# Middle units numbered by chunk, the first bias transposed by TensorE, another order on VectorE in the first layer, and two of four shared rounded copies made by VectorE

## The chip, the cores and the metric

The kernel runs on one core of one Trainium2 chip. The time is device microseconds of one execution; three executions of the kernel before gave 276.58, 276.78 and 278.21 us, median 276.78. The profile is of a fourth execution, taken by the hardware profiler.

## The reference

Two layers with residuals, for 32 batches of 128 tokens with 128 features. What is computed, cut to its core:

```python
# layer 0: a dense layer plus a low-rank term that differs by batch
z = ((x @ v) / 128) @ u.T / 16                # u = v = fside, 128 x 16 per batch
x = x + gelu(x @ W.T + fc_bias + z + cond)    # exact gelu
# layer 1: a gate picks 2 of 4 experts per batch, and a shared expert is always added
logits = gate_in @ gate_w + gate_b            # gate_in: three means over token segments of x
w_be = top-2 softmax weights of logits * (1 + scale) + shift     # scale, shift from cond
for e in range(4):                            # expert 1 skips one token segment, expert 2 another
    h = gelu_tanh(x @ ew1[e] + eb1[e])        # 128 -> 512
    out += w_be[e] * mask[e] * (h @ ew2[e] + eb2[e])             # 512 -> 128
x = x + out + (gelu_tanh(x @ sw1 + sb1) @ sw2 + sb2)
```

The order of the 512 middle units is free, as long as the first weights' columns, the first bias and the second weights' rows agree.

## The kernel before, in words

Features lie on the partitions. The 32 batches are 8 tiles of 4 batches (512 token columns). Tokens are reordered into three segments so that each expert reads one contiguous range: the shared expert (s = 0) and experts s = 1 and 4 take 512 columns per tile, s = 2 and 3 take 344.

Every product of layer 1 is done as three matmuls of values split into a rounded part and a rest (lines 449 to 451, `product3`: high by high, low by high, high by low). So each weight matrix is rounded by ScalarE (`weight_high`, line 323) and its rest is taken by VectorE (`weight_low`, line 679), and each middle activation `h` is split into `hs_hi` and `hs_lo`.

The work of layer 1 is a list `STEPS` of (tile, expert). It begins (0,0), (1,0), then the four experts of tile 0, then (2,0), the four experts of tile 1, (3,0), and so on: a round is four expert steps and one shared step. A step k has three parts:

- `up(k)` on TensorE: 4 chunks of 128 middle units, three matmuls each, into a ring of five PSUM banks. Chunk n waits until ScalarE has finished chunk n-5 (`h_ok`). TensorE runs `up` two steps ahead of `down`.
- `gelu(k)` on ScalarE: one activation per chunk into `h` (line 373). In a shared step a second activation per chunk writes the rounded `hs_hi` straight from PSUM (line 376). Before a shared step it waits until `down(k-2)` is done (line 370), as that frees `hs_hi`; before any step it waits for the split of step k-3 (line 368).
- `split(k)` on VectorE: for an expert `hs_hi` = h * w_be (line 695) and `hs_lo` (line 700), four instructions each; for a shared step only `hs_lo`, two instructions over two chunks each (line 689). Then `down(k)` on TensorE waits for `lo_ok`.

Layer 0 is done for tiles 0 to 3 ahead of layer 1 (xT, transpose_F, matrices, layer0 on TensorE; matrix, residual on VectorE; gelu0 on ScalarE). The first layers of tiles 4 to 7 are woven into rounds 0 to 3 (`late_tile`). In those rounds ScalarE loads another activation table, does `gelu0_late` (lines 354 to 361) and loads the first table again, right behind the shared step. The gate of tiles 0 to 3 is computed by VectorE (`segment_sums`, `time_gate`, `gate_in`, `modulation`, `gate_logits`, `gate_weights`, `output_biases`) with two small matmuls (lines 604 and 576) and one tanh on ScalarE; tiles 4, 5 and 6, 7 follow in later rounds.

Each engine's instructions stand in the order in which the code writes them, and wait by semaphores; nothing is reordered. SyncE issues nearly all loads in one queue: inputs, then weights in the order `WEIGHTS = [0, 1, 2, 4, 3, 6, 5, 8, 7, 9]` (2s is the first matrix of expert s, 2s+1 the second). Middle unit numbers are p * 4 + c for chunk c: the first matrices are read with a stride of four elements (line 201), and each partition of a second matrix is one run of 2 KB (line 249). GpSimd adds the output biases to `x1`, three instructions per tile (line 308), as soon as `output_biases` of the tile's gate group is done; `out_sum(t)` on VectorE waits for them.

## Time and profile before

| | |
|---|---|
| median of three runs | 276.78 us |
| profiled execution | 276.94 us, of which its span 274.8 us |
| TensorE (PE) busy | 244.4 us, 89% |
| VectorE (DVE) busy | 198.8 us, 72% |
| ScalarE (ACT) busy | 156.2 us, 57% |
| GpSimd (POOL) busy | 22.2 us, 8% |
| mean granted TensorE clock | 0.958 of 2.4 GHz |

How to read it: the profile cuts the span in 40 slices of 6.9 us and gives each engine's busy share and the granted clock of TensorE by slice in tenths. The timeline of one engine lists its instructions in order with the idle time before each and the engine that ended it. TensorE's modelled busy time reaches past the start of the next matmul; the distance from start to start is what a matmul costs in a stream.

### The profile page before, as it was taken

Reading aid. Unit: us, or ns where it says so; the run is one execution under the profiler, and the core shown is the slowest. Engines: PE = TensorE matmul, PEld = TensorE weight load, DVE = VectorE, ACT = ScalarE, POOL = GpSimd, SP = SyncE. Lnnn points to the kernel's source line nnn. Section 1 sums busy time; section 2 is a strip of 40 time slices with the busy share of each in tenths; the row PEclk is TensorE's granted clock in tenths of the full one; section 3 lists DMA queues with packets and bytes.
Section 4 is the critical chain, followed back from the end, with each engine's and each line's share of the span. In section 5 each row is a group of like instructions: output and inputs, shape, how many; then the busy total and the mean of one; then the engine's idle time right before and its main releaser. Section 6 shows DMA issues by size and latency. Waiting matters only on the chain.

```text
span 274.8 us, 3451 instructions
## 1 busy us (share of the span) xinstructions
PE 244.4 (89%) x1217; PEld 203.2 (74%) x1217; DVE 198.8 (72%) x441; ACT 156.2 (57%) x286; POOL 22.2 (8%) x39
## 2 busy tenths in 40 slices
PE   8964969799979997999989997999979989999963
PEld 7763748678768875888768885887768959898852
DVE  0266799999369565797399795797499959779661
ACT  4375799630894439760894439751835194544400
POOL 5000000940000000000000060000000600000000
PEclk9995598999999999999999999999999999999987
DMA  6995000000001000010001000010001000100101
GB/s 129 235 284 96 1 1 0 0 2 0 0 2 38 0 0 4 6 32 2 1 0 38 2 0 0 6 36 0 0 0 41 0 0 0 43 0 0 38 0 38
DMA packets 15811, 7.40 MB, mean 27 GB/s; under 512 B 6175, under 2 KB 14515, under 8 KB 15795
## 3 DMA queue, kind: packets, MB, share of 16 engines
q1 hardware_dynamic: 14781, 6.98, 10.6%
q10 hardware_dynamic: 854, 0.18, 0.3%
q8 instruction: 9, 0.15, 0.2%
q0 software_dynamic: 160, 0.02, 0.1%
q14 instruction: 7, 0.06, 0.1%
HBM read 5.09 MB, written 2.10 MB: 26 GB/s over the span
## 4 chain that ended last, share of the span: by engine, by line
PE 61%; ACT 16%; DVE 14%; issue 4%; DMA 2%; SPq 2%; DVEq 0%; ACTq 0%
PE ps L449 19%; PE ps L451 17%; PE ps L450 17%; ACT h L373 5%; ACT hs_hi L376 4%; DVE hs_lo L700 4%; DVE hs_hi L695 3%; PE ps L496 2%; DMA x_tok<-in_x 2%; DVE W_lo L679 2%; ACT L373 2%; ACT L354 2%; PE ps L508 2%; DVE hs_lo L689 2%; ACT W_raw L359 2%
## 5 line engine op out<-in xcount | busy, mean ns | idle before, releaser
L373 ACT ACTIVATE h<-ps,b_col 128x512 f32<-128x512 f32 (+1 forms) x160 | 94.1, 649 | 60.5 <-PE ps L451 38.4
L700 DVE SCALAR_TENSOR_TENSOR hs_lo<-h,w_be,hs_hi 128x512 fp32r<-128x512 f32 (+1 forms) x128 | 78.4, 673 | 0.0
L449 PE MATMUL ps<-x_hi,W_hi 128*128 128x512 f32 (+1 forms) x160 | 65.1, 407 | 14.2 <-ACT h L373 5.5
L449 PE MATMUL ps<-hs_hi,W_hi 128*128 128x512 f32 (+1 forms) x160 | 59.9, 375 | 6.3 <-DVE hs_lo L700 4.9
L695 DVE TENSOR_SCALAR hs_hi<-h,w_be 128x512 fp32r<-128x512 f32 (+1 forms) x128 | 50.3, 455 | 13.7 <-ACT h L373 6.9
L451 PE MATMUL ps<-x_lo,W_hi 128*128 128x512 f32 (+1 forms) x160 | 60.0, 375 | 0.0
L450 PE MATMUL ps<-x_hi,W_lo 128*128 128x512 f32 (+1 forms) x160 | 59.8, 374 | 0.0
L451 PE MATMUL ps<-hs_lo,W_hi 128*128 128x512 f32 (+1 forms) x160 | 59.0, 369 | 0.0
L450 PE MATMUL ps<-hs_hi,W_lo 128*128 128x512 f32 (+1 forms) x160 | 59.0, 369 | 0.0
L449 PEld LDWEIGHTS ps<-x_hi,W_hi 128*128 128x128 f32 x160 | 30.8, 192 | 27.9 <-ACT hs_hi L376 10.8
L449 PEld LDWEIGHTS ps<-hs_hi,W_hi 128*128 128x128 f32 x160 | 30.6, 191 | 11.6 <-DVE hs_lo L700 2.8
L689 DVE TENSOR_TENSOR hs_lo<-h,hs_hi 128x1024 fp32r<-128x1024 f32 x16 | 18.9, 1221 | 24.8 <-ACT hs_hi L376 24.8
L451 PEld LDWEIGHTS ps<-x_lo,W_hi 128*128 128x128 f32 x160 | 30.9, 193 | 4.5
L308 POOL TENSOR_TENSOR x<-x,bias 128x168 f32<-128x168 f32 (+1 forms) x24 | 18.2, 789 | 196.6 <-DVE bias L812 196.6
L451 PEld LDWEIGHTS ps<-hs_lo,W_hi 128*128 128x128 f32 x160 | 30.6, 191 | 4.3
L450 PEld LDWEIGHTS ps<-hs_hi,W_lo 128*128 128x128 f32 x160 | 30.7, 192 | 4.2
L450 PEld LDWEIGHTS ps<-x_hi,W_lo 128*128 128x128 f32 x160 | 31.1, 194 | 3.1
L376 ACT ACTIVATE hs_hi<-ps,b_col 128x512 fp32r<-128x512 f32 x32 | 22.8, 711 | 0.0
L391 ACT ACTIVATE x_tok<-ps 128x512 f32<-128x512 f32 x8 | 4.8, 598 | 28.6 <-PE ps L562 28.6
L327 ACT ACTIVATE x<-ps 128x512 f32<-128x512 f32 x8 | 4.8, 597 | 17.9 <-PE ps L466 17.9
L712 DVE TENSOR_TENSOR outT<-ps,x 128x168 f32<-128x168 f32 (+1 forms) x24 | 6.5, 327 | 5.3 <-PE ps L451 5.2
L654 DVE SCALAR_TENSOR_TENSOR h<-ps,WT 128x512 f32<-128x512 f32 x4 | 2.8, 689 | 9.3 <-PE ps L496 9.3
(102 smaller groups left out, 173.4 us busy)
## 6 DMA issues: line engine op xcount, KB each, us to landing
W_raw<-in_L_cond_ew SPq DMA_DIRECT2D x8, 256.0 KB, 4.9
out<-x_tok SPq DMA_DIRECT2D x8, 256.0 KB, 2.3
x_tok<-in_x SPq DMA_DIRECT2D x6, 168.0 KB
x_tok<-in_x SPq DMA_DIRECT2D x3, 176.0 KB
W_raw<-in_L_cond_sw SPq DMA_DIRECT2D x2, 256.0 KB, 5.0
x_tok<-in_x SPq DMA_DIRECT2D x3, 84.0 KB
F_raw<-in_fside_Bx1x1024x SPq DMA_DIRECT2D x3, 64.0 KB, 5.3
x_tok<-in_x SPq DMA_DIRECT2D x2, 88.0 KB
```

Source lines behind the costliest of these rows:

```text
L308: nc.gpsimd.tensor_tensor(xb[:, :, at:at + n], xb[:, :, at:at + n], bias2[:, i, t * NB:(t + 1) * NB].unsqueeze(2).to_broadcast([128, NB, n ...
L354: nc.scalar.activation(table_probe[:, 1:2], table_probe[:, 0:1], ACT.Gelu)
L359: ins = nc.scalar.activation(g0_late[:, b * L:(b + 1) * L], psLate[:, b * L:(b + 1) * L], ACT.Gelu, bias=bias0[:, t * NB + b:t * NB + b + 1])
L373: ins = nc.scalar.activation(span(h[:, k % 3, c, :], s), up_bank(k, c), ACT.Gelu_apprx_tanh, bias=b1_col[:, s, c:c + 1])
L376: ins = nc.scalar.activation(hs_hi[:, k % 2, c, :], up_bank(k, c), ACT.Gelu_apprx_tanh, bias=b1_col[:, s, c:c + 1])
L449: nc.tensor.matmul(dst, w_hi, m_hi, start=start, stop=False)
L450: nc.tensor.matmul(dst, w_lo, m_hi, start=False, stop=False)
L451: return nc.tensor.matmul(dst, w_hi, m_lo, start=False, stop=stop)
L689: nc.vector.tensor_tensor(hs_lo[:, k % 2, c:c + 2, :], h[:, k % 3, c:c + 2, :], f32(hs_hi[:, k % 2, c:c + 2, :]), ALU.subtract).then_inc(l ...
L695: nc.vector.tensor_scalar(hs_hi[:, k % 2, :, c], h[:, k % 3, :, c], w_be[:, t * NB + b, s - 1:s], None, ALU.mult).then_inc(hi_ok, 1)
L700: nc.vector.scalar_tensor_tensor(hs_lo[:, k % 2, :, c], h[:, k % 3, :, c], w_be[:, t * NB + b, s - 1:s], f32(hs_hi[:, k % 2, :, c]), ALU.m ...
L712: nc.vector.tensor_tensor(dst_v[:, :, dst:dst + n], sum_v[:, :, at:at + n], x1_v[:, :, at:at + n], ALU.add).then_inc(outT_ok, 1)
```

## The change

Six edits:

1. Middle units are numbered c * 128 + p. The first matrices are then read contiguously by the casts; a second matrix is loaded as four runs of 512 B per partition.
2. The first biases are loaded as 20 rows of 512 B (`b1_rows`), earlier in SyncE's queue, transposed by TensorE into PSUM (behind the transpose of `eb2`), and copied into `b1_col` by VectorE.
3. VectorE's order in the first layer: the block `segment_sums(0, 2)`, `time_gate`, `output_rows` no longer stands ahead of the matrix of tile 3. `weight_low` of the first matrix, `x1_low` and others move with it; `output_biases(0)` moves behind the split of step 4; two `weight_low` now stand ahead of `gate_logits(0)`.
4. TensorE: six idle matmuls ahead of `up(0)`; the modulation matmul behind `up(0)` instead of ahead of it; `logits(0)` behind `up(1)` instead of `up(0)`. ScalarE rounds the fourth weight ahead of `gelu(0)` instead of behind `gate_tanh(0)`.
5. In a shared step ScalarE writes `hs_hi` of chunks 0 and 1 only; VectorE copies chunks 2 and 3 from `h` in one instruction of 1024 columns.
6. GpSimd's bias additions of tile t also wait until VectorE's split of the step two before the tile's first expert step is done.

```diff
-                return W1_raw[:, e, :].rearrange("p (m c) -> p c m", c=CH), W1_hi[:, e, :, :], W1_lo[:, e, :, :]
+                return W1_raw[:, e, :].rearrange("p (c m) -> p c m", c=CH), W1_hi[:, e, :, :], W1_lo[:, e, :, :]
...
-                    sp.dma_start(W2_raw[:, e, :], src.rearrange("(p c) d -> p (c d)", c=CH)).then_inc(w_in[n], 16)
+                    sp.dma_start(W2_raw[:, e, :].rearrange("p (c d) -> p c d", c=CH),
+                                 src.rearrange("(c p) d -> p c d", c=CH)).then_inc(w_in[n], 16)
...
             load_weight(WEIGHTS[0])
+            sp.dma_start(b1_rows[0:CH, :], sb1.rearrange("(c p) -> c p", c=CH)).then_inc(b1_in, 16)
+            sp.dma_start(b1_rows[CH:NS * CH, :], eb1.rearrange("e (c p) -> (e c) p", c=CH)).then_inc(b1_in, 16)
...
             for t in range(NT):
+
+                pool.wait_ge(lo_ok, parts_until(first_step(t) - 2))
                 pool.wait_ge(bias2_ok, next(g for g, (a, z) in enumerate(GATES) if a <= t < z) + 1)
...
-                    if s == 0:
+                    if s == 0 and c < CH // 2:
                         ins = nc.scalar.activation(hs_hi[:, k % 2, c, :], up_bank(k, c), ACT.Gelu_apprx_tanh,
...
-            act.wait_ge(b1_in, 32)
+            weight_high(WEIGHTS[3])
+            act.wait_ge(b1_ok, 1)
             gelu(0)
             gate_tanh(0)
-            weight_high(WEIGHTS[3])
             gelu(1)
...
+                    pe.wait_ge(b1_in, 16 * 2)
+                    nc.tensor.transpose(psB1, b1_rows[:, :], ident[0:NS * CH, 0:NS * CH]).then_inc(b1_ps, 1)
+
+            keep_busy(6, ps[:, 6, 0:128])
+            up(0)
             pe.wait_ge(eb2T_read, NSEG)
+            pe.wait_ge(b1_ok, 1)
             pe.wait_ge(mod_terms_ok, 1)
             nc.tensor.matmul(psMod, ones[:, :], mod_terms[:, :, :], start=True, stop=True).then_inc(mod_ps, 1)
-            up(0)
+            up(1)
             logits(0)
-            up(1)
...
                 if s == 0:
+
+                    nc.vector.tensor_copy(hs_hi[:, k % 2, CH // 2:, :], h[:, k % 3, CH // 2:, :]).then_inc(shared_hi_ok, 1)
                     for c in range(0, CH, 2):
+                        if c == CH // 2:
+                            dve.wait_ge(shared_hi_ok, t + 1)
...
+                dve.wait_ge(b1_ps, 1)
+                nc.vector.tensor_copy(b1_col[:, :, :], psB1.rearrange("p (s c) -> p s c", c=CH)).then_inc(b1_ok, 1)
...
-                if t == 1:
+                if t == 2:
+                    output_rows()
+                    weight_low(WEIGHTS[0])
                     segment_sums(0, 2)
-                    time_gate()
-                    output_rows()
-            weight_low(WEIGHTS[0])
             segment_sums(2, 4)
+            time_gate()
             gate_in(0)
+            x1_low(NA - 1)
             dve.wait_ge(bias_in, 16 * 3)
             modulation()
-            x1_low(NA - 1)
-            gate_logits(0)
             weight_low(WEIGHTS[1])
             weight_low(WEIGHTS[2])
+            gate_logits(0)
...
-            output_biases(0)
...
+                if k == 4:
+                    output_biases(0)
```

Two places in the order of instructions. First VectorE in the first layer, before, from the rest of x1 of tile 0 on (`h<-ps,WT` is the matrix of a tile, `x<-x,h` its residual, `x_lo` the rest of its x1):

```order
L666 TENSOR_TENSOR x_lo<-x,x_hi 128x512
L673 TENSOR_REDUCE segsum<-x 128x8 x3
L717 SCALAR_TENSOR_TENSOR silu<-tanh_c,condT 128x32
L720 TENSOR_SCALAR tw<-time_w_raw 128x8
L722 TENSOR_TENSOR mod_terms<-silu,tw 128x256
...
L736 COPY eb2T<-ps 128x4 x3
L738 MEMSET eb2T 128x1
L739 MEMSET eb2T 128x1
L654 SCALAR_TENSOR_TENSOR h<-ps,WT 128x512
L661 TENSOR_TENSOR x<-x,h 128x512
L666 TENSOR_TENSOR x_lo<-x,x_hi 128x512
```

and the same place now:

```order
L678 TENSOR_TENSOR x_lo<-x,x_hi 128x512
L666 SCALAR_TENSOR_TENSOR h<-ps,WT 128x512
L673 TENSOR_TENSOR x<-x,h 128x512
L678 TENSOR_TENSOR x_lo<-x,x_hi 128x512
L752 COPY eb2T<-ps 128x4 x3
L754 COPY b_col<-ps 128x20
L756 MEMSET eb2T 128x1
L757 MEMSET eb2T 128x1
L691 TENSOR_TENSOR W_lo<-W_raw,W_hi 128x512
L685 TENSOR_REDUCE segsum<-x 128x8 x3
L673 TENSOR_TENSOR x<-x,h 128x512
```

The matrix of tile 3 (the `h<-ps,WT` row) now follows the rest of tile 0 directly, and the rest of the first weight stands ahead of all sums.

Second ScalarE around the first shared step, before, from the last cast of x1 on:

```order
L382 ACTIVATE x_hi<-x 128x512
L323 ACTIVATE W_hi<-W_raw 128x512
L373 ACT_TABLE_LOAD
L373 ACTIVATE h<-ps,b_col 128x512
L376 ACTIVATE hs_hi<-ps,b_col 128x512
L373 ACTIVATE h<-ps,b_col 128x512
L376 ACTIVATE hs_hi<-ps,b_col 128x512
L373 ACTIVATE h<-ps,b_col 128x512
L376 ACTIVATE hs_hi<-ps,b_col 128x512
L373 ACTIVATE h<-ps,b_col 128x512
L376 ACTIVATE hs_hi<-ps,b_col 128x512
L386 ACTIVATE tanh_g<-logit_x 128x64
```

and now:

```order
L389 ACTIVATE x_hi<-x 128x512
L330 ACTIVATE W_hi<-W_raw 128x512 x2
L380 ACT_TABLE_LOAD
L380 ACTIVATE h<-ps,b_col 128x512
L383 ACTIVATE hs_hi<-ps,b_col 128x512
L380 ACTIVATE h<-ps,b_col 128x512
L383 ACTIVATE hs_hi<-ps,b_col 128x512
L380 ACTIVATE h<-ps,b_col 128x512 x2
L393 ACTIVATE tanh_g<-logit_x 128x64
```

Six activations stand where eight stood, here and in each of the other seven shared steps, and one more weight is rounded ahead of them.

## Rows read from the trace of the kernel before

**Rows 1.** The page: granted TensorE clock in 40 slices, tenths of full speed.

```profile
PEclk9995598999999999999999999999999999999987
```

**Rows 2.** Timeline of TensorE: start, us, line, tiles, count, idle before and who ended it.

```profile
17.39 1.16 PE L508 MATMUL ps<-x,h 128*128 128x128 f32 x8
22.54 2.05 PE L508 MATMUL ps<-x,h 128*128 128x128 f32 x8 [3.99 <-issue]
...
28.12 0.80 PE L449 MATMUL ps<-x_hi,W_hi 128*128 128x512 f32 x1 [2.68 <-DVE W_lo L679]
...
55.59 0.47 PE L449 MATMUL ps<-hs_hi,W_hi 128*128 128x512 f32 x1 [2.37 <-DVE hs_lo L700]
```

**Rows 3.** Timeline of VectorE in the first 52 us.

```profile
18.73 1.33 DVE L673 TENSOR_REDUCE segsum<-x 128x8 f32<-128x336 f32 x3
...
21.74 0.69 DVE L654 SCALAR_TENSOR_TENSOR h<-ps,WT 128x512 f32<-128x512 f32 x1
...
25.79 0.69 DVE L661 TENSOR_TENSOR x<-x,h 128x512 f32<-128x512 f32 x1 [2.16 <-ACT h L348]
...
33.77 0.23 DVE L766 TENSOR_TENSOR logit<-ps,gate_mul 128x64 f32<-128x64 f32 x1 [1.69 <-PE ps L576]
...
46.76 0.69 DVE L679 TENSOR_TENSOR W_lo<-W_raw,W_hi 128x512 fp32r<-128x512 f32 x1
47.36 0.50 DVE L808 TENSOR_TENSOR gate_terms<-w_be,eb2T 128x64 f32<-128x64 f32 x3
...
48.45 1.07 DVE L679 TENSOR_TENSOR W_lo<-W_raw,W_hi 128x512 fp32r<-128x512 f32 x1
49.44 2.48 DVE L695 TENSOR_SCALAR hs_hi<-h,w_be 128x512 fp32r<-128x512 f32 x4
51.84 3.60 DVE L700 SCALAR_TENSOR_TENSOR hs_lo<-h,w_be,hs_hi 128x512 fp32r<-128x512 f32 x4
```

**Rows 4.** Timeline of GpSimd, and of VectorE in a later round.

```profile
48.62 9.69 POOL L308 TENSOR_TENSOR x<-x,bias 128x168 f32<-128x168 f32 x12 [43.45 <-DVE bias L812]
...
127.08 1.67 DVE L695 TENSOR_SCALAR hs_hi<-h,w_be 128x512 fp32r<-128x512 f32 x4
128.66 2.73 DVE L700 SCALAR_TENSOR_TENSOR hs_lo<-h,w_be,hs_hi 128x512 fp32r<-128x512 f32 x4
```

**Rows 5.** Timeline of ScalarE in the first layer: the table load of the first shared step.

```profile
29.85 1.28 ACT L373 ACT_TABLE_LOAD   x1 [1.54 <-PE ps L451]
```

**Rows 6.** Timeline of ScalarE in two rounds: first and last activation of a shared step.

```profile
69.81 0.69 ACT L373 ACTIVATE h<-ps,b_col 128x512 f32<-128x512 f32 x1 [7.28 <-PE ps L451]
...
100.61 0.69 ACT L373 ACTIVATE h<-ps,b_col 128x512 f32<-128x512 f32 x1 [7.28 <-DVE hs_lo L700]
...
104.61 0.73 ACT L376 ACTIVATE hs_hi<-ps,b_col 128x512 fp32r<-128x512 f32 x1
```

**Rows 7.** Timeline of TensorE in the same round, in the third, and after the last first layer.

```profile
108.11 0.32 PE L451 MATMUL ps<-x_lo,W_hi 128*128 128x344 f32 x1
109.94 0.43 PE L449 MATMUL ps<-x_hi,W_hi 128*128 128x344 f32 x1 [1.51 <-ACT h L373]
...
140.74 0.43 PE L449 MATMUL ps<-x_hi,W_hi 128*128 128x344 f32 x1 [0.97 <-ACT h L373]
...
194.77 0.50 PE L449 MATMUL ps<-x_hi,W_hi 128*128 128x512 f32 x1 [0.19 <-ACT hs_hi L376]
...
202.03 0.50 PE L449 MATMUL ps<-hs_hi,W_hi 128*128 128x512 f32 x1 [1.40 <-DVE outT L712]
```

**Rows 8.** Timeline of TensorE: two matmuls in a stream at the full clock.

```profile
96.36 0.39 PE L449 MATMUL ps<-x_hi,W_hi 128*128 128x512 f32 x1
96.59 0.39 PE L450 MATMUL ps<-x_hi,W_lo 128*128 128x512 f32 x1
```

**Rows 9.** Two stretches: length, busy us of PE, PEld, DVE, ACT, POOL, clock, DMA share, GB/s.

```profile
14.00:17.00 3.00, 3.00 (x27) 2.68 (x26) 1.29 (x2) 2.20 (x7) 0.00 (x0) 1.00 1.01 373
22.50:24.50 2.00, 1.97 (x9) 2.00 (x10) 1.13 (x2) 0.00 (x0) 0.00 (x0) 0.50 0.84 170
```

More of the change, by code:

```diff
@@ L73, in build @@
         eb2_raw = sb("eb2_raw", [E, D])
+        b1_rows = sb("b1_rows", [NS * CH, 128])
         b1_col = sb("b1_col", [128, NS, CH])
@@ L142, in build @@
                                                               sem("probe_ok"), sem("before_ok"))
+        b1_ps, b1_ok = sem("b1_ps"), sem("b1_ok")
         xT_ps, fT_ps, M_ps, y_ps = sem("xT_ps"), sem("fT_ps"), sem("M_ps"), sem("y_ps")
@@ L155, in build @@
             sem("tanh_g_ok"), sem("w_ok"), sem("bias2_ok"), sem("x1b_ok"))
+        shared_hi_ok = sem("shared_hi_ok")
         up_ps, h_ok, hi_ok, lo_ok, down_ok = sem("up_ps"), sem("h_ok"), sem("hi_ok"), sem("lo_ok"), sem("down_ok")
@@ L169, in build @@
         psMod = ps[:, 7, 256:256 + 2 * E * B].rearrange("p (b e) -> p b e", e=2 * E)
+        psB1 = ps[:, 7, 224:224 + NS * CH]
         psLogit = ps[:, 7, 0:B * E].rearrange("p (b e) -> p b e", e=E)
@@ L262, in _ @@
             load_weight(WEIGHTS[1])
-            sp.dma_start(b1_col[:, 0, :], sb1.rearrange("(p c) -> p c", c=CH)).then_inc(b1_in, 16)
-            sp.dma_start(b1_col[:, 1:NS, :], eb1.rearrange("e (p c) -> p e c", c=CH)).then_inc(b1_in, 16)
             for n in WEIGHTS[2:]:
@@ L451, in product3, with keep_busy @@
                 return nc.tensor.matmul(dst, w_hi, m_lo, start=False, stop=stop)
-            def keep_busy(n):
+            def keep_busy(n, dst=psIdle):
                 for _ in range(n):
-                    nc.tensor.matmul(psIdle, ones[:, :], ones[:, :], start=True, stop=True)
+                    nc.tensor.matmul(dst, ones[:, :], ones[:, :], start=True, stop=True)
             def xT(t):
```

## The prediction

> **What bounds the kernel now.** I read the clock line of the page first, then the timeline of TensorE for its idle times, then the engine that each names. The clock is at half in the fourth and fifth slice (20.6 to 34.4 us), dips in the seventh, and is full from there to the last slices [rows 1]. From 55.6 us on TensorE works nearly without a break; its work sets the time there, and only what it waits for can be won. Two regions hold the waits.
>
> The head, up to the first matmul of `down(2)` at 55.59. TensorE stands idle 3.99 us ahead of layer 0 of tile 3, 2.68 us ahead of `up(0)`, and 2.37 us ahead of `down(2)` [rows 2]. The profile calls the first "issue"; the code says that this matmul waits for the matrix of tile 3, which VectorE makes at 21.74, behind a block of sums and gate terms that begins at 18.73 [rows 3]. The last two waits name VectorE outright. VectorE itself is idle only twice between 18.73 and 55.5, for 2.16 and 1.69 us [rows 3]. So VectorE's own queue is the head's length, and I sum over it.
>
> The rounds. In a shared step ScalarE starts at 100.61. The profile names line 700 of VectorE as the releaser there, but the same step one round earlier names TensorE [rows 6]. Line 370 makes it wait for `down(k-2)`, and I take that for the releaser in both. So it is a loop: TensorE frees ScalarE, ScalarE does eight activations, a table load, the four of `gelu0_late`, a table load and one activation, and TensorE's ring of banks waits for that one: it starts a matmul at 108.11 and the next at 109.94 [rows 7], 1.83 us apart where 0.16 is the distance in that stream. 1.67 us is lost.
>
> **The change part by part.**
>
> Head, on VectorE's queue, to the start of `down(2)`:
>
> - The matrix of tile 3 moves from 21.74 to 18.73. Layer 0 of tile 3 then starts near 19.4 instead of 22.54, `gelu0(3)` ends near 21.9 and no longer leaves VectorE idle: minus 2.16.
> - `gate_logits(0)` starts when TensorE's logits come. I follow them: residual of tile 3 at 23.5 (behind the moved sums), then on ScalarE a cast of x1, two of weights and the table load of 1.28 [rows 5], first gelu at 27.1; chunks 0 and 1 take 1.15 each, chunk 2 0.57. `up(1)` chunk 3 needs chunk 2, done near 30.0, and logits follow at 31.0. VectorE meanwhile does modulation and two `weight_low`, until 31.05. So the idle time of 1.69 shrinks to some 0.25: minus 1.45.
> - Four first matrices have their `weight_low` in the stretch. A strided one takes 1.07, a contiguous one 0.69 [rows 3], and from its start to the next instruction 0.99 against 0.60: minus 1.5.
> - `output_biases(0)`, 47.36 to 48.45 [rows 3], goes behind step 4: minus 1.1.
> - The split of step 2 runs from 49.44 beside GpSimd's twelve additions (0.81 each) and needs 2.48 and 3.60; without them 1.67 and 2.73 [rows 3, 4]. The additions now come later: minus 1.7.
> - Added: two copies of 1024 columns. Not in the trace; the nearest row is four TENSOR_SCALAR of 512 in 1.67, so 0.42 each, which grows with columns to 0.65; at the pace of a two-input instruction it would be 1.15. I take 0.65, as copy and TENSOR_SCALAR both read one tensor: plus 1.3, bound 2.3.
> - The bias copy of 20 columns from PSUM and its transpose: plus 0.15, bounds 0 and 0.5.
>
> Sum: 2.16 + 1.45 + 1.5 + 1.1 + 1.7 - 1.3 - 0.15 = 6.5 us; `down(2)` starts near 49.1. TensorE's part must fit: from the split of step 0 (near 37.5) it has two `down` and `up(3)`, `up(4)`, 12 matmuls each, 0.23 apart for 512 columns [rows 8] and 0.16 for 344, and each `down` or `up` waits for a VectorE result of its own; at the full clock it is ready at 48.8, just in time. At half clock, which rows show after thin stretches (the same eight passes 2.05 instead of 1.16 [rows 2]), it is late by 0.5 to 2. TensorE's work between 26 and 37 will be thin, as it waits for gelus chunk by chunk, and the clock fell after such stretches before [rows 1]. I take 0.5 off: head 6.0, bounds 4.2 and 6.7.
>
> What follows `down(2)` on TensorE is bound by its own stream until the first shared step at 69.81, as before. The displaced `output_biases(0)` and the first three additions lie ahead of the split of step 5, which is wanted near 67.5 and done by 65: covered by over 2 us. Were that cover gone, it would cost 1.1 plus some 0.6 of slowed VectorE.
>
> On GpSimd: the rows show a VectorE instruction slowed by about 0.2 beside an addition. The Trainium skill, SBUF — State Buffer, on the shared port pair, calls it an exclusive lock, the loser blocked for a whole instruction. By that the split of step 2 would have lost up to 6 us, not 1.7; the trace disagrees, and the sum keeps the rows. In the rounds the additions now run while VectorE waits for the shared gelus, so they cost nothing.
>
> Rounds: ScalarE loses two activations per shared step, each 0.57 from start to start (100.61 to 104.61 are seven) [rows 6]: 1.15. In rounds 0, 1 and 3 all of it reaches TensorE, since 1.67 is lost there: 3 x 1.15. In the third the loss is less (0.97 idle [rows 7]), and `out_sum` stands behind the gate's logits on VectorE: 0.9. In the two shared steps without a late first layer only the last chunk's wait goes: chunk 3 starts at 194.77 behind the gelus of chunk 2 [rows 7], 0.46 earlier now, and the wait of 1.40 at 202.03 behind it hangs on the same logits and moves along: 2 x 0.46. Sum 5.3, bounds 3.5 and 6. VectorE's copy begins 1.15 earlier and lasts 0.65, so the shared split ends 0.5 earlier than now; even at 1.15 it ends no later. Its `down` comes 3 us later: covered.
>
> ScalarE's casts: shorter, inside waits, beyond what is counted nothing. DMA: a second matrix now comes in pieces of 512 B. The stretch with 2 KB pieces moved 373 GB/s, one of mostly 512 B pieces 170 [rows 9]. Five matrices of 256 KB take 3.5 us at the one and 7.7 at the other: loads end 4 us later, near 28 us; the last weights are cast after 40 and tile 4 is wanted near 48. Hidden, 0. The Trainium skill, DMA: Bandwidth & Descriptors, gives 512 B as enough for line rate, which would make it 0 for another reason; the rows show half the rate. The bias rows are issued ahead of where they were, near 7 us, and wanted at 16.3. If late, they would hold TensorE with all of layer 0 behind them.
>
> **Total.** 6.0 + 5.3 = 11.3. The profiled execution took 276.9, its span 274.8; the median of the runs is 0.2 lower. 276.9 - 11.3 = 265.6.
>
> **The rivals.**
>
> - *The half clock eats head gain* (0.2): `up(1)`, `up(2)` and `down(0)` run at 1.2 GHz and logits come 1.6 later, `down(2)` near 51 or later. Head 3 to 4, total 267.6 to 268.6. For: thin work from 26 to 37. Against: a dense stretch restored the clock before [rows 1].
> - *The rounds give half* (0.12): a wait that I don't see, most likely `out_sum` or VectorE's longer shared step, takes the place of the ring's wait. 2.5 instead of 5.3: 268.4.
> - *The edits don't do what they say in the head* (0.06): VectorE's gelu or logits wait stays, or the copies run at the two-input pace; 3 us of head: 268.6 to 271.
> - *More is won* (0.12): the end of the kernel, at half clock in the last slices [rows 1], falls in another phase, and the head stays at full clock: 2 us more, 263.
> - *Slower* (0.02): the half clock lasts. After the thin head TensorE is kept at 1.2 GHz into the rounds. Each microsecond of dense work costs half of one, so it takes over 22 us of stretch beyond what it has now to use up 11.3, and 28 for 1%: 280. The longest such stretch in the trace is two slices; so it is unlikely.
>
> My forecast (0.48): 264.0 to 267.2. Weights together leave under 2 in 10 outside 262.5 to 269.0: past 269 lie part of the third rival, the slow one and combinations; under 262.5 part of the fourth.
>
> A measurement here tells 1% from no change, 2.8 us: faster means under 274.0. All but the last rival are; with something left for errors that I don't see, 0.95 faster, 0.03 same, 0.02 slower.
>
> **What would show it.** Layer 0 of tile 3 on TensorE near 19.5; `up(0)` near 22.4; first gelu on ScalarE near 27; VectorE idle under 0.5 ahead of the logits; a strided `W_lo` of 1.06 nowhere; the copy of 1024 columns at 0.6 to 0.7; the split of step 2 at 4.3 in all; `down(2)` near 49; from one shared step to the next 29.7 instead of 30.8; TensorE's ring wait of 1.51 down to 0.4. I am wrong if VectorE is idle for over 2 us between 31 and 49, if the clock is at half through 37 to 49, or if a round stays at 30.8.

## The result, and the profile after

The changed kernel took 263.73 us (median of four executions, 262.72 to 265.1) against 277.24 us for the kernel before beside it: a ratio of 0.951, interval 0.945 to 0.957. Six more executions on another occasion gave 263.33 us and the ratio 0.951 (0.947 to 0.956). The profiled execution took 262.98 us, its span 261.3. So the change made it faster by some 13.5 us where 11.3 were forecast; 263.73 lies inside the range of 262.5 to 269.0, but just under the band of 264.0 to 267.2 that the forecast held most likely (0.48), and nearest to the 263 of the rival *More is won* (0.12). In the tables below, the positions are those of the profiled executions.

The clock line of the changed kernel's page, in the same 40 slices as [rows 1]:

```profile
PEclk9999979999999999999999999999999999999999
```

The half clock between 20.6 and 34.4 us is gone but for one slice (32.7 to 39.2 us), and so are the lower digits of the last two slices.

TensorE's timeline after, in the head; its columns are those of [rows 2]:

```profile
19.01 1.13 PE L515 MATMUL ps<-x,h 128*128 128x128 f32 x8 [0.91 <-issue]
...
21.73 0.50 PE L456 MATMUL ps<-x_hi,W_hi 128*128 128x512 f32 x1 [0.25 <-DVE W_lo L691]
...
33.37 0.78 PE L456 MATMUL ps<-x_hi,W_hi 128*128 128x512 f32 x1 [1.78 <-ACT hs_hi L383]
...
48.77 0.47 PE L456 MATMUL ps<-hs_hi,W_hi 128*128 128x512 f32 x1
```

These answer to the 22.54, 28.12 and 55.59 rows of [rows 2]: layer 0 of tile 3 comes 3.5 us earlier, `up(0)` 6.4 and `down(2)` 6.8. The idle 2.37 us ahead of `down(2)` are gone. A matmul of 512 columns takes 0.78 us at 33.37, which is the half clock: TensorE worked there at 1.2 GHz, behind 1.78 us of idleness.

VectorE's timeline after, over the stretch of [rows 3]:

```profile
18.23 0.68 DVE L666 SCALAR_TENSOR_TENSOR h<-ps,WT 128x512 f32<-128x512 f32 x1
...
20.98 0.69 DVE L691 TENSOR_TENSOR W_lo<-W_raw,W_hi 128x512 fp32r<-128x512 f32 x1
...
30.88 0.22 DVE L784 TENSOR_TENSOR logit<-ps,gate_mul 128x64 f32<-128x64 f32 x1 [0.34 <-PE ps L583]
...
34.17 0.69 DVE L701 CAST hs_hi<-h 128x1024 fp32r<-128x1024 f32 x1
34.78 2.36 DVE L705 TENSOR_TENSOR hs_lo<-h,hs_hi 128x1024 fp32r<-128x1024 f32 x2
...
44.31 1.67 DVE L711 TENSOR_SCALAR hs_hi<-h,w_be 128x512 fp32r<-128x512 f32 x4
45.90 2.73 DVE L716 SCALAR_TENSOR_TENSOR hs_lo<-h,w_be,hs_hi 128x512 fp32r<-128x512 f32 x4
```

The wait of 2.16 us for the gelu of tile 3 has no successor, the one of 1.69 us before the logits is 0.34. `W_lo` takes 0.69 us. The added copy of 1024 columns takes 0.69, 0.61 to the next start. The split of step 2 takes 1.67 and 2.73 where it took 2.48 and 3.60, because GpSimd's first additions now start here, behind it:

```profile
58.65 1.77 POOL L315 TENSOR_TENSOR x<-x,bias 128x168 f32<-128x168 f32 x3 [53.46 <-DVE bias L830]
```

ScalarE's timeline after, three shared steps: the third, the fourth and the last of the kernel ([rows 6] has the first two of them before):

```profile
62.99 0.69 ACT L380 ACTIVATE h<-ps,b_col 128x512 f32<-128x512 f32 x1 [7.26 <-PE ps L458]
...
92.62 0.69 ACT L380 ACTIVATE h<-ps,b_col 128x512 f32<-128x512 f32 x1 [7.26 <-DVE hs_lo L716]
...
208.16 0.69 ACT L380 ACTIVATE h<-ps,b_col 128x512 f32<-128x512 f32 x1 [6.00 <-PE ps L458]
```

and TensorE's: the last chunk of the shared `up` at 92.62, the ring's wait behind it, and the last `down`:

```profile
95.91 0.39 PE L456 MATMUL ps<-x_hi,W_hi 128*128 128x512 f32 x1
...
100.81 0.43 PE L456 MATMUL ps<-x_hi,W_hi 128*128 128x344 f32 x1 [0.81 <-ACT h L380]
...
253.32 0.50 PE L456 MATMUL ps<-hs_hi,W_hi 128*128 128x512 f32 x1 [2.55 <-DVE hs_lo L716]
```

The kernel before has these for the last shared step on ScalarE, and on TensorE for the last chunk of the shared `up` at 100.61 and for the last `down`:

```profile
219.72 0.69 ACT L373 ACTIVATE h<-ps,b_col 128x512 f32<-128x512 f32 x1 [6.00 <-PE ps L451]
```

```profile
104.24 0.50 PE L449 MATMUL ps<-x_hi,W_hi 128*128 128x512 f32 x1 [0.20 <-ACT hs_hi L376]
...
265.34 0.68 PE L449 MATMUL ps<-hs_hi,W_hi 128*128 128x512 f32 x1 [2.54 <-DVE hs_lo L700]
```

The same four positions, read off every profile, cut the span in four parts. `A` is the start of the third shared step on ScalarE, at 69.81 before and 62.99 after:

| profile | A | A to last shared step | from there to last `down` | last `down` to end | span |
|---|---|---|---|---|---|
| before | 69.81 | 149.91 | 45.62 | 9.5 | 274.8 |
| after | 62.99 | 145.17 | 45.16 | 8.0 | 261.3 |
| difference | -6.82 | -4.74 | -0.46 | -1.5 | -13.5 |

Head 6.8 (forecast 6.0), rounds 4.7 and 0.5 (forecast 5.3), and 1.5 at the end, for which the forecast had no term: the last `down` of the execution before began at half clock (0.68 us for 512 columns), the one after did not (0.50).

Not all of the head's 6.8 us is won where the forecast looked for it. A second profile of the changed kernel (the repeat among the experiments) has its first layer later from the start. Its VectorE at the residual ahead of the moved matrix, and its TensorE at `down(2)`:

```profile
17.61 0.69 DVE L673 TENSOR_TENSOR x<-x,h 128x512 f32<-128x512 f32 x1 [1.71 <-ACT h L355]
```

```profile
49.38 0.47 PE L456 MATMUL ps<-hs_hi,W_hi 128*128 128x512 f32 x1
```

That residual starts at 17.01 in the first profile and at 17.52 in the kernel before. From it to `down(2)` it is 31.8 us in both profiles of the changed kernel and 38.1 before. So 6.3 us are won behind the residual, where the edits are, and the other 0.5 is an earlier start that one execution of the changed kernel had and the other had not.

### The profile page after: what moved, and what is told of

It reads as the page before. It is cut to its first block, busy times and chain, and to the rows that moved or that the text cites. A ratio compares the mean times of both kernels' runs of the same rounds, so it can differ in the third digit from the quotient of the medians.

```text
span 261.3 us, 3479 instructions
## 1 busy us (share of the span) xinstructions
PE 240.2 (92%) x1230; PEld 200.7 (77%) x1230; DVE 196.7 (75%) x450; ACT 145.0 (55%) x270; POOL 15.1 (6%) x39
## 4 chain that ended last, share of the span: by engine, by line
PE 67%; ACT 14%; DVE 14%; issue 3%; DVEq 0%; POOL 0%; ACTq 0%; POOLq 0%
PE ps L456 20%; PE ps L458 18%; PE ps L457 18%; ACT h L380 5%; PE ps L503 3%; DVE hs_lo L716 3%; ACT hs_hi L383 3%; DVE hs_lo L705 2%; ACT L380 2%; DVE hs_hi L711 2%; PE ps L473 2%; PE ps L462 2%; PE ps L487 2%; ACT L361 1%; PE ps L569 1%
## 5 line engine op out<-in xcount | busy, mean ns | idle before, releaser
L380 ACT ACTIVATE h<-ps,b_col 128x512 f32<-128x512 f32 (+1 forms) x160 | 92.4, 642 | 64.1 <-PE ps L458 49.4
L716 DVE SCALAR_TENSOR_TENSOR hs_lo<-h,w_be,hs_hi 128x512 fp32r<-128x512 f32 (+1 forms) x128 | 76.2, 656 | 0.0
L456 PE MATMUL ps<-x_hi,W_hi 128*128 128x512 f32 (+1 forms) x160 | 64.3, 402 | 8.2 <-ACT hs_hi L383 4.9
L456 PE MATMUL ps<-hs_hi,W_hi 128*128 128x512 f32 (+1 forms) x160 | 59.2, 370 | 5.2 <-DVE hs_lo L716 2.5
L458 PE MATMUL ps<-x_lo,W_hi 128*128 128x512 f32 (+1 forms) x160 | 59.0, 369 | 0.0
L457 PE MATMUL ps<-hs_hi,W_lo 128*128 128x512 f32 (+1 forms) x160 | 58.2, 363 | 0.0
L711 DVE TENSOR_SCALAR hs_hi<-h,w_be 128x512 fp32r<-128x512 f32 (+1 forms) x128 | 48.2, 440 | 12.7 <-PE ps L458 6.7
L315 POOL TENSOR_TENSOR x<-x,bias 128x168 f32<-128x168 f32 (+1 forms) x24 | 11.1, 490 | 213.4 <-DVE hs_lo L716 159.9
L701 DVE CAST hs_hi<-h 128x1024 fp32r<-128x1024 f32 x8 | 5.5, 693 | 20.2 <-ACT h L380 20.2
L383 ACT ACTIVATE hs_hi<-ps,b_col 128x512 fp32r<-128x512 f32 x16 | 11.0, 689 | 0.0
```

The costliest lines, as they stand in the source:

```text
L315: nc.gpsimd.tensor_tensor(xb[:, :, at:at + n], xb[:, :, at:at + n], bias2[:, i, t * NB:(t + 1) * NB].unsqueeze(2).to_broadcast([128, NB, n ...
L380: ins = nc.scalar.activation(span(h[:, k % 3, c, :], s), up_bank(k, c), ACT.Gelu_apprx_tanh, bias=b1_col[:, s, c:c + 1])
L383: ins = nc.scalar.activation(hs_hi[:, k % 2, c, :], up_bank(k, c), ACT.Gelu_apprx_tanh, bias=b1_col[:, s, c:c + 1])
L456: nc.tensor.matmul(dst, w_hi, m_hi, start=start, stop=False)
L457: nc.tensor.matmul(dst, w_lo, m_hi, start=False, stop=False)
L458: return nc.tensor.matmul(dst, w_hi, m_lo, start=False, stop=stop)
```

## Experiments

Ratios are against the kernel before, run beside each kernel on the same chip, with 95% intervals; the changed kernel stands at 0.951 in both of its comparisons.

**Each edit undone.** First the shared copies back on ScalarE (edit 5):

```diff
-                    if s == 0 and c < CH // 2:
+                    if s == 0:
...
-                    nc.vector.tensor_copy(hs_hi[:, k % 2, CH // 2:, :], h[:, k % 3, CH // 2:, :]).then_inc(shared_hi_ok, 1)
```

> The changed kernel with edit 5 undone: ScalarE writes all four rounded copies of a shared step, VectorE none. Theory A (ScalarE's shared step sits in a loop with TensorE's ring): from one shared step of a late first layer to the next 30.8 us again instead of 29.6, TensorE's ring wait back to 1.5 from 0.8, rounds 5.3 us longer; in the head VectorE saves two copies of 0.6 but the logits come 0.6 later, so 0.6 is given back; in all 4.7 us more, about 268.5. Theory B (VectorE's copy costs as much as ScalarE saves, and the rounds' gain came from elsewhere, GpSimd's moved additions for one): within 1 us of the changed kernel, 263 to 264.5.

Measured 268.81 us, 0.970 (0.966 to 0.974). Its TensorE and ScalarE rows:

```profile
102.65 0.43 PE L456 MATMUL ps<-x_hi,W_hi 128*128 128x344 f32 x1 [1.53 <-ACT h L380]
```

```profile
62.52 0.69 ACT L380 ACTIVATE h<-ps,b_col 128x512 f32<-128x512 f32 x1 [7.26 <-PE ps L458]
...
212.40 0.69 ACT L380 ACTIVATE h<-ps,b_col 128x512 f32<-128x512 f32 x1 [6.00 <-PE ps L458]
```

The ring's wait is 1.53 us again (1.51 in [rows 7]), and from shared step to last shared step it is 149.88 us, within 0.03 of before. The head stays short: edit 5 carries all of the rounds' gain and none of the head's. Undone, it even gives the head 0.5, or 0.8 counted from the residual, which starts 0.3 later here (17.30).

VectorE's order and TensorE's places for the modulation and the logits are one edit in two halves; this undoes the main part of VectorE's half alone, the place of the block of sums, time gate and output rows and that of the first `weight_low`:

```diff
+                dve.wait_ge(b1_ps, 1)
...
-                if t == 2:
+                if t == 1:
+                    segment_sums(0, 2)
+                    time_gate()
                     output_rows()
-                    weight_low(WEIGHTS[0])
-                    segment_sums(0, 2)
+            weight_low(WEIGHTS[0])
             segment_sums(2, 4)
-            time_gate()
```

> The changed kernel with the block of sums, time gate and output rows back ahead of the matrix of tile 3 on VectorE, and the rest of the first weight behind all residuals. Theory A (the matrix of tile 3 was late behind that block): layer 0 of tile 3 on TensorE at 22 instead of 19.0, VectorE idle again for about 2 us ahead of the residual of tile 3, down(2) 2.2 to 3.2 us later; about 266.5. Theory B (VectorE's sum of work sets the head whatever its order): under 0.7 us more, 264.

Measured 268.39 us, 0.968 (0.962 to 0.975): more than expected. Its page, its TensorE and its VectorE:

```profile
PEclk9995688999999999999999999999999999999999
```

```profile
22.00 2.05 PE L515 MATMUL ps<-x,h 128*128 128x128 f32 x8 [3.93 <-issue]
```

```profile
25.26 0.69 DVE L673 TENSOR_TENSOR x<-x,h 128x512 f32<-128x512 f32 x1 [2.16 <-ACT h L355]
...
32.72 0.42 DVE L762 TENSOR_TENSOR mod<-ps,time_b_row 128x256 f32<-128x256 f32 x1 [2.92 <-PE ps L617]
```

The idle 3.93 us on TensorE and 2.16 us on VectorE are those of [rows 2, 3], to within 0.1. But a new wait of 2.92 us appears, which neither kernel has: the modulation matmul stands behind `up(0)`, and `up(0)` is late and at half clock. So VectorE's old order doesn't go with TensorE's new one, and this undo (4.95 us at A) costs more than the gain it takes back.

`output_biases(0)` early again, and GpSimd's wait taken out (edit 6 and the end of edit 3):

```diff
-                pool.wait_ge(lo_ok, parts_until(first_step(t) - 2))
...
             weight_low(WEIGHTS[4])
+            output_biases(0)
             weight_low(WEIGHTS[5])
...
-                if k == 4:
-                    output_biases(0)
```

> The changed kernel with the output biases of the first gate group computed before the split of step 2 and GpSimd's additions without the added wait, so all twelve run at once then. Theory A (they lie on VectorE's chain, 1.1 us, and GpSimd slows the split of step 2 by 1.7): down(2) 2.8 us later, 266.5. Theory B (only the order of VectorE's work counts, the slowing is hidden): 1.1 us later, 264.8. Theory C (neither on the path): no change, 263.7.

Measured 268.77 us, 0.967 (0.959 to 0.974), with executions from 265.44 to 271.4. VectorE and TensorE at step 2:

```profile
45.16 2.53 DVE L709 TENSOR_SCALAR hs_hi<-h,w_be 128x512 fp32r<-128x512 f32 x4
47.61 3.59 DVE L714 SCALAR_TENSOR_TENSOR hs_lo<-h,w_be,hs_hi 128x512 fp32r<-128x512 f32 x4
```

```profile
51.35 0.47 PE L454 MATMUL ps<-hs_hi,W_hi 128*128 128x512 f32 x1 [2.88 <-DVE hs_lo L714]
```

`down(2)` starts 2.6 us later (2.8 with the 0.2 by which this execution's tile 3 came sooner), which is the forecast's 1.1 + 1.7. The surplus is behind it: after 2.88 us of idleness the matmuls go to half clock within 1.5 us. The stretch from 53 to 56 in its table of stretches (columns as in [rows 9]) has the clock at 0.50:

```profile
53.00:56.00 3.00, 3.00 (x10) 2.31 (x9) 3.00 (x7) 0.00 (x0) 0.81 (x2) 0.50 0.00 0
```

From the start of `down(2)` to A it is 15.8 us instead of the 14.2 of both main kernels, so the clock takes 1.6 of the 4.2 us by which A is late; and this profile's last `down` is at half clock too (9.5 us to the end, not 8.0).

The same biases early, but GpSimd's wait kept, so that only three additions lie beside the split:

> The changed kernel with the output biases of the first group back ahead of the split of step 2, but GpSimd's additions still waiting tile by tile, so that only three of twelve run beside the splits. With the run that took both away it parts edit 6 from the order. Theory A (the slowing is by instruction that overlaps): 1.1 for the biases and 0.5 for three additions, down(2) 1.6 later, 265. Theory B (GpSimd's presence at the start of the split is all that counts): the same 2.8 as with both undone, 266.2.

Measured 266.33 us, 0.958 (0.953 to 0.963). VectorE, GpSimd and TensorE:

```profile
46.70 2.32 DVE L711 TENSOR_SCALAR hs_hi<-h,w_be 128x512 fp32r<-128x512 f32 x4
48.95 2.73 DVE L716 SCALAR_TENSOR_TENSOR hs_lo<-h,w_be,hs_hi 128x512 fp32r<-128x512 f32 x4
```

```profile
46.35 2.00 POOL L315 TENSOR_TENSOR x<-x,bias 128x168 f32<-128x168 f32 x3 [41.16 <-DVE bias L830]
```

```profile
51.82 0.48 PE L456 MATMUL ps<-hs_hi,W_hi 128*128 128x512 f32 x1 [1.79 <-DVE hs_lo L716]
```

GpSimd is done at 48.35, and the second half of the split, from 48.95, takes its undisturbed 2.73. The first half loses 0.65. So the slowing belongs to the instructions that overlap: 0.65 for three additions; 1.7 in the run before, where twelve additions took from 44.73 to 53.81 us and some eight of them lay beside the split. That is 0.2 us per addition both times. The median is the one that theory B gave, but not for its reason. This profile is of the slowest of the four executions (267.64; the fastest took 264.64), and its clock was between 0.50 and 0.77 in most of the stretch from 28 to 38 us: the logits came late (VectorE idle for 1.46 us instead of 0.34), and `down(2)` started 3.05 us late, of which 1.1 are the biases, 0.65 the additions, 1.1 the logits and 0.2 the start. It was 0.57 again from 52 to 56, behind the 1.79 us of idleness. The interval also touches that of the changed kernel (0.945 to 0.957), so by time alone even the cost of this undo is not clear of noise.

Numbering by chunk and the bias by transpose (edits 1 and 2) undone, all else kept:

```diff
-                return W1_raw[:, e, :].rearrange("p (c m) -> p c m", c=CH), W1_hi[:, e, :, :], W1_lo[:, e, :, :]
+                return W1_raw[:, e, :].rearrange("p (m c) -> p c m", c=CH), W1_hi[:, e, :, :], W1_lo[:, e, :, :]
...
+            sp.dma_start(b1_col[:, 0, :], sb1.rearrange("(p c) -> p c", c=CH)).then_inc(b1_in, 16)
```

> The changed kernel with edits 1 and 2 undone: middle units numbered p * 4 + c, strided casts of the first matrices, second matrices in pieces of 2 KB, biases loaded straight into columns by 16-byte packets. Theory A (strided reads cost VectorE 0.38 us each, four before down(2)): 1.5 us less the bias copy of 0.15, plus up to 0.5 if the 16-byte packets hold up the first inputs (down(2) 1.4 to 1.9 later): about 265.4. Theory B (they were hidden, and the larger pieces help): 263.7 or less.

Measured 268.17 us, 0.968 (0.963 to 0.973). VectorE here, then ScalarE here, then ScalarE of the changed kernel:

```profile
21.02 1.09 DVE L687 TENSOR_TENSOR W_lo<-W_raw,W_hi 128x512 fp32r<-128x512 f32 x1
...
32.29 0.23 DVE L778 TENSOR_TENSOR logit<-ps,gate_mul 128x64 f32<-128x64 f32 x1 [0.95 <-PE ps L582]
```

```profile
24.53 2.11 ACT L329 ACTIVATE W_hi<-W_raw 128x512 fp32r<-128x512 f32 x2
```

```profile
24.10 1.13 ACT L330 ACTIVATE W_hi<-W_raw 128x512 fp32r<-128x512 f32 x2
```

Its head is 2.4 us longer, 2.3 counted from the residual: the strided rest costs 0.4 more each on VectorE, and two strided casts 1.0 more on ScalarE, just ahead of the first table load, so that the logits come later too (0.95 of idleness, not 0.34). I had taken ScalarE's casts for hidden; they are on the path once VectorE's block is gone. The rest of the profiled execution's difference, 1.5, is again an end at half clock.

The six idle matmuls ahead of `up(0)` (edit 4) taken out:

```diff
-            keep_busy(6, ps[:, 6, 0:128])
             up(0)
```

> The changed kernel without the six idle matmuls ahead of up(0). Theory A (they keep the clock at full through up(0) and the modulation): half clock from about 20 us in the records, up(0) at 0.43 a matmul, its gelus still bound by ScalarE's table load, so 0 to 1.5 us more, 263.5 to 265. Theory B (they do nothing for the clock): the same records as the changed kernel, 263.3.

Measured 264.44 us, 0.952 (0.949 to 0.955). TensorE:

```profile
21.72 0.50 PE L456 MATMUL ps<-x_hi,W_hi 128*128 128x512 f32 x1 [1.59 <-DVE W_lo L690]
```

TensorE is idle for 1.59 us instead of 0.25, and nothing follows: `up(0)` is at full clock, A is at 62.99 as with them, the span 261.2. In the trace they do nothing. The median is 0.7 above the changed kernel's, which theory A would allow, but the intervals overlap and the trace shows nothing of that theory's half clock.

**One edit alone.** The kernel before with edit 5 only:

> The kernel before with edit 5 alone: ScalarE writes two rounded copies of a shared step, VectorE the other two. Theory A (the rounds' gain is this edit's alone and adds up with the head's): rounds 5.3 us shorter, head longer by two copies of 0.6 less 0.6 for logits that come sooner: 4.5 us less than before, 272.4. Theory B (without GpSimd's added wait VectorE is too slow, and the gain needs both): under 2.5 us gained, 274.5 or more.

Measured 273.79 us, 0.986 (0.982 to 0.990). TensorE and ScalarE:

```profile
56.06 0.47 PE L450 MATMUL ps<-hs_hi,W_hi 128*128 128x512 f32 x1 [3.22 <-DVE hs_lo L704]
57.37 0.63 PE L451 MATMUL ps<-hs_hi,W_lo 128*128 128x512 f32 x1
```

```profile
71.87 0.69 ACT L374 ACTIVATE h<-ps,b_col 128x512 f32<-128x512 f32 x1 [7.29 <-DVE hs_lo L704]
...
217.01 0.69 ACT L374 ACTIVATE h<-ps,b_col 128x512 f32<-128x512 f32 x1 [6.00 <-PE ps L452]
```

The rounds take 145.14 us, the whole 4.8 of the gain without GpSimd's wait. The head pays: the copies delay `down(2)` by 0.5, TensorE stands idle 3.22 us instead of 2.37, and now the clock falls behind it (0.63 us per matmul), so that A is 2.06 late. That is why the edit alone brings 1.4%, less than theory A's 4.5 us: the rounds follow theory A, the head does not.

**Further along the same way.** If ScalarE's share of a shared step is what the ring waits for, more of it should go to VectorE. All four chunks copied there from the third shared step on; the first stays at two, the second returns to ScalarE:

```diff
+    HI_ACT = [2 if k == 0 else 4 if k == 1 else 0 for k in range(K)]
...
-                    if s == 0 and c < CH // 2:
+                    if s == 0 and c < HI_ACT[k]:
```

> The changed kernel, but from the third shared step on VectorE makes all four rounded copies in one instruction of 2048 columns; in the second shared step ScalarE makes all four, since VectorE is the head's bound there. Theory A (ScalarE is still the longer side of the loop in a round, its ring wait of 0.8 and the chunk waits are all its): 1.15 less in three rounds, 0.5 in the one with the gate's logits, 1.1 in the two without a late first layer, 0.6 in the head: 6 to 6.5 us less than the changed kernel, 257.5. Theory B (VectorE takes over as bound, its shared split being 0.55 longer in work): under 2 us gained, 262 or more.

Measured 256.51 us, 0.926 (0.923 to 0.930). VectorE and TensorE:

```profile
65.08 1.23 DVE L704 CAST hs_hi<-h 128x2048 fp32r<-128x2048 f32 x1 [1.70 <-ACT h L381]
```

```profile
98.10 0.43 PE L457 MATMUL ps<-x_hi,W_hi 128*128 128x344 f32 x1 [0.21 <-ACT h L381]
...
129.50 0.50 PE L457 MATMUL ps<-hs_hi,W_hi 128*128 128x512 f32 x1 [1.03 <-DVE outT L732]
...
185.04 0.50 PE L457 MATMUL ps<-hs_hi,W_hi 128*128 128x512 f32 x1 [1.41 <-DVE outT L732]
```

The ring's wait is down to 0.21 and the rounds, from the shared step at 62.62 to the last at 202.72, to 140.10 us. What is left names `outT`: the matmul waits for VectorE's output sum, which stands behind the gate's logits. So the sums were put ahead of the logits:

```diff
-                if s == NS - 1:
+                if s == NS - 1 and late_gate(k - 1, 4) is None:
                     out_sum(t)
...
                 if g is not None:
+                    out_sum(STEPS[k - 1][0])
                     gate_logits(g)
```

> The kernel with all copies on VectorE from the third shared step (256.5), and in the two rounds where a gate group's logits lie ahead of the output sums of a tile on VectorE, the sums first. Theory A (TensorE's waits of 1.03 and 1.41 at a shared down are for those sums, behind 2.5 us of logits): both waits go, 2.4 to 2.8 us less, 254. Theory B (the logits then come late for someone): 255.5 or more.

Measured 255.88 us, 0.922 (0.918 to 0.925), the fastest kernel of the study. TensorE, the second row beside the 185.04 of the kernel above, and the page's clock:

```profile
187.85 0.50 PE L457 MATMUL ps<-hs_hi,W_hi 128*128 128x512 f32 x1 [0.43 <-DVE hs_lo L720]
...
244.51 0.68 PE L457 MATMUL ps<-hs_hi,W_hi 128*128 128x512 f32 x1 [2.54 <-DVE hs_lo L720]
```

```profile
PEclk9997999999999999999999999999999999999977
```

Both `outT` waits are gone, as theory A has it, and the rounds (62.42 to 200.39) take 137.97 us, 2.1 less; of this the medians show 0.6 and the ratios 1.3, and the profiled execution ended at half clock, which gives 1.5 back. The intervals of the two kernels overlap, so the gain of this last step is shown by the positions, not by the times, which would fit theory B as well.

**The end, and repeatability.** The changed kernel again:

> The changed kernel as it is, for comparison on this chip: theory A (the last down runs at the full clock in some executions and at half in others): times in two groups about 2 us apart, 262.8 and 264.8, and a ratio of 0.951 to 0.957 to the kernel before. Theory B (one level with noise): a single spread around 263.7.

263.57, 263.27, 263.38, 262.86, 265.83 and 262.93 us. Five lie together, one is 2.5 above; the four of the first comparison lay at 262.72, 262.98, 264.48 and 265.1. The two groups that I expected are only hinted at. The idle 2.5 us ahead of the last `down` filled with nine idle matmuls:

```diff
+                if k == K - 1:
+                    keep_busy(9, psY[0][:, 0:128])
                 down(k)
```

> The changed kernel with nine idle matmuls put ahead of the last down, where TensorE stands idle for 2.55 us. Theory A (the idle time lets the clock fall in some executions, for 1.5 to 2 us of the last down): every execution near 262.8, spread under 1 us. Theory B (the spread has another origin): the same two groups as the changed kernel.

Measured 263.07 us, 0.949 (0.946 to 0.952). TensorE:

```profile
253.31 0.50 PE L456 MATMUL ps<-hs_hi,W_hi 128*128 128x512 f32 x1 [0.53 <-DVE hs_lo L718]
```

The idle time is 0.53 and the executions spread over 1.15 us instead of 2.97, but the intervals overlap. Both this and all copies on VectorE:

> Both: all copies on VectorE from the third shared step on, and the idle matmuls ahead of the last down. By theory A of each, 256.5 with a small spread; if VectorE becomes the bound, 262.

Measured 256.71 us, 0.928 (0.924 to 0.933), no gain over the copies alone, and one execution of it took 259.89. So the fill is not shown to help, and the idle time ahead of the last `down` is not the whole cause of the spread.

## Why the prediction was right

**VectorE's queue as the length of the head** held by its steps. Layer 0 of tile 3 was forecast near 19.4 and stands at 19.01, `up(0)` near 22.4 and at 21.73, the first gelu at 27.1 and 26.54, the idle time before the logits 0.25 and 0.34, the strided `W_lo` gone, the copy 0.65 and 0.61, the split of step 2 at 4.3 and 4.24, `down(2)` near 49.1 and at 48.77. The two undo experiments priced two terms apart: biases and additions 2.8 us, exactly the sum's 1.1 + 1.7; the numbering 2.4, of which the sum had 1.5 on VectorE and nothing on ScalarE.

**The head was mis-sized by 0.8 in the profile, by 0.3 in the stretch that the sum is about.** Of the 6.8 us, 0.5 is the early start of the profiled execution. The forecast had no term for it, and the second profile of the same kernel doesn't have it. The residual starts at 17.52 and 17.62 in the two profiles with the old order (before, and edit 5 alone) and between 16.80 and 17.30 in the others but that second one (17.61). The kernel with the old numbering and the old loads is among them (17.11), so the start is not a gift of the loads; whether it is one of another edit or chance stays open. The 6.3 behind the residual lie between the forecast's 6.0 and the 6.5 that its sum had before I took off 0.5 for the half clock, and that half microsecond was not paid. The clock did fall, from 33.4 to about 37 us, as TensorE's thin `up(2)` ran. The kernel with early biases has the same instructions up to there and kept the full clock; TensorE then stood idle ahead of `down(0)`:

```profile
37.07 0.47 PE L454 MATMUL ps<-hs_hi,W_hi 128*128 128x512 f32 x1 [1.09 <-DVE hs_lo L703]
```

Its first layer came 0.2 sooner, so this is the changed kernel's 37.28. The half clock used up an idle time that was there anyway, because `down(0)` waits for VectorE.

**GpSimd beside VectorE** went as the rows said: a two-input instruction 0.90 instead of 0.68, by overlap alone, 0.2 us per addition. Three additions that take 1.33 us when nothing runs beside them (at 92.68 in the changed kernel) cost VectorE 0.65. The Trainium skill, SBUF — State Buffer, on the shared port pair, which would block the loser for a whole instruction, asks for more than any trace here shows.

**The rounds** held at 5.2 against 5.3. Step by step too: the five stretches between shared steps are 1.17, 1.17, 0.82, 1.13 and 0.45 us shorter, and the last stretch to the last `down` 0.46. Undoing edit 5 gave all of it back, and it alone brought all of it. The reading that a shared step waits for `down(k-2)`, though the profile names VectorE in some rounds, was right as well, and a step where the two part shows it. TensorE's last matmul of `down(k-2)` and VectorE's split of step k-1, before:

```profile
69.40 0.32 PE L451 MATMUL ps<-hs_lo,W_hi 128*128 128x344 f32 x1
```

```profile
67.56 2.73 DVE L700 SCALAR_TENSOR_TENSOR hs_lo<-h,w_be,hs_hi 128x512 fp32r<-128x512 f32 x4
```

ScalarE starts at 69.81, 0.09 behind that matmul and 0.48 ahead of the split's end. In all six shared steps from there on, before and after, it starts 0.08 to 0.09 us behind that matmul; in the rounds where the profile names VectorE, the split happens to end in the same tenth.

One size was off: the ring's wait stays at 0.81, not 0.4. The forecast took the whole 1.15 off it. But TensorE waits for ScalarE earlier in the same step too, ahead of the last chunk of the shared `up`: from the start of the step on ScalarE to that chunk it is 3.63 us before (104.24) and 3.29 after (95.91), where the wait is gone. With the slower first matmul behind it, 0.44 of the gain falls there and 0.70 in the ring's wait. The forecast saw this wait in the steps without a late first layer and missed it in the others; the sum stayed right, as ScalarE bounds both.

**The step that the sum lacked** is the end. The forecast had it in a rival (another phase of the clock, 0.12) and not in the sum. From the start of the last `down` to the end the profiles show 7.9 to 8.0 us where it runs at full clock, 8.6 in the kernel with edit 5 alone, where only its last matmuls are at half clock, and 9.2 to 9.5 in the five in which all or more than half of it is: before, all copies on ScalarE, early biases with the additions, old numbering, and sums first. Kernels with the same idle time of 2.54 us ahead of it show both levels, and so do kernels that have the change; what sets the level stays open. By medians the change gives 13.5 us all the same, so the 1.5 may be in part the chance of the executions that were profiled. In the profiles this 1.5 and the early start of 0.5 are 2.0 of the 2.2 us by which the gain exceeds the forecast's 11.3, and no term of the sum explains them; why the medians exceed it as much is not shown. The time fell where the rival *More is won* had it, but of its two causes the full clock in the head did not come.

**What undoing taught about adding.** The undo experiments cost 5.1, 4.7, 5.0, 2.6 and 4.4 us by median (copies, order, biases with additions, biases alone, numbering; the third 4.9 without its execution of 271.4), and the last four cost more than their terms in the sum. With the order it is the new wait of 2.92 us. With the biases TensorE stands idle ahead of `down(2)` and pays for it again in clock: from there to A it is 15.8 us instead of 14.2, 1.6 more, behind 2.88 us of idleness as behind 1.79, and as in the kernel with edit 5 alone behind 3.22. With the numbering it is ScalarE's casts and an end at half clock. The changed kernel has none of these in its head, and so none of the surplus.

**The loads had a wrong price, and it didn't matter.** The forecast let them end 4 us later, near 28 us, because a stretch of mostly 512 B pieces had moved 170 GB/s [rows 9]. They ended as before: from 8 to 24 us both kernels moved 245 GB/s, from 24 to 25 us 115 before and 77 after, and nothing from 26 to 28. The kernel with the old numbering, whose second matrices come in runs of 2 KB, moved 244 GB/s from 8 to 24 us, and 163 from 21 to 23 where the changed kernel moved 159. So the slow stretch is there with either length of piece, and the change from 2 KB to 512 B cost these loads nothing that shows.

## What to carry to other kernels

Find the engine that the waits name and sum over its queue; a term there is worth its whole length until TensorE's own work becomes the limit. Where two engines feed each other in a loop, work moved off the slower one is won in full each round, so go on moving it until another wait stands in its place, and then look at what that wait stands behind. Price an idle time ahead of a dense matmul stretch with the clock that it may cost, which an experiment that undoes one edit pays as well.

## What the runs showed of the hardware

The length of one idle time did not tell what the clock did behind it. Behind 2.37 us [rows 2] and 1.59 us the matmuls were at full speed, behind 1.79, 2.88 and 3.22 us they went to half, and the last `down` behind 2.54 us was at either level. Nor did the code: the changed kernel, the one with early biases and the one with the biases alone have the same instructions up to the split of step 2, and the first fell to half at 33.37 behind 1.78 us, the second stayed at full speed behind 1.77 us at the same place, and the third had fallen at 28.06, behind 0.35 us. Six idle matmuls before `up(0)` changed nothing in the trace.

A copy of fp32 to fp32r on VectorE takes 0.69 us for 1024 columns and 1.23 for 2048, 0.6 to 0.7 ns per column, where a two-input instruction takes 0.69 for 512. A stride of four words in its input costs VectorE 0.4 us per 512 columns (1.07 to 1.09 against 0.69) and ScalarE 0.5 (two casts 2.11 against 1.13).
